# GpSimd's scatters and gathers in both expert layers, without their waits on TensorE's steps

## The chip, the core and the metric

The kernel runs on one core of a Trainium2 chip. TensorE (PE), VectorE (DVE), ScalarE (ACT) and GpSimd (POOL) compute, and transfers run on 16 DMA engines. They are issued by SyncE (SP) and, where rows are picked by an index in memory, by GpSimd as indirect DMAs. The metric is the device time of one execution in microseconds, the median over the runs shown.

## The reference

Sixteen sequences of 512 tokens with 256 features go through four layers, each added to its input after a layer norm: attention a, a mixture of experts, attention b, and the same mixture of experts again. The expert layer, cut to what matters here:

```python
logits = flat @ Wg.T                       # 16 experts
topk_idx, topk_w = _route(sigmoid(logits), bias_corr)   # 4 experts per token
hid = relu(flat @ W1[e].T) ** 2
y = hid @ W2[e].T
out = sum over the token's 4 experts of topk_w * y
shared = relu(flat @ Ws1.T) ** 2 @ Ws2.T
return out + shared
```

## The kernel before

The program has four phases behind one another, with a barrier between them: `phase_a` (attention a), `phase_f` (first expert layer), `phase_b` (attention b, with the routing of the second expert layer) and `phase_e` (second expert layer). In the profiled execution `phase_f` takes roughly from 805 to 1440 us and `phase_e` from 2127 us to the end.

An expert layer computes only the chosen experts. The rows of a sequence are copied to `slots` in DRAM, sorted by expert (a scatter), the sorted rows are worked on in steps of 4 tiles of 128 rows, the results go to `made` in DRAM, and each token's four results are fetched back (a gather), weighted and added by VectorE (`combine`). A block is 128 tokens; a block's scatter or gather is 4 indirect DMAs of 128 rows of 1 KB, one for each of the 4 chosen experts. A sequence has 4 blocks.

One step `v` of tiles is, over the engines:

- SP: `load_tiles(v)` brings 512 KB of `slots` to `xg` (4 buffers), `store_tiles(v)` brings 512 KB of `ye` (2 buffers) to `made`. Both stand in one order in SP's queue, so that a load waits behind the store in front of it.
- PE: `tile_turn(v)` transposes to `XT`, `tile_hidden(v)` makes `Z` (semaphore `ze_done`), `tile_made(v)` makes `Y` (`ye_done`).
- ACT and DVE: copies of expert weights to `wt`, of `XT` to `xe`, relu and square of `Z`, copies of `Y` to `ye`.

Each engine runs the same hand-written loop over slots of time `T`. In slot `T`, step `v = T - E_AT` stands on PE as turn of `v + 1`, hidden of `v`, made of `v - 1`; `E_AT` is 18 in `phase_f` and 2 in `phase_e`. Work of the router, of the shared expert and the combining is put in fixed slots between. Nothing but semaphores keeps the engines in the same slot.

`phase_f` has 84 steps, in 5 groups of sequences (2, 2, 4, 4, 4). When a group is routed, VectorE writes its positions (`pack`, semaphore `packed`, L1391), and GpSimd scatters its blocks, one per slot `T` of `LOT_AT`. The gathers of sequences 0 and 1 are done here too, in the slots from `G_AT`, the ones of the others in `phase_b`. In `phase_f` the waits at issue are `in_step` (on the router's products in the slots ahead of the first step of tiles) and `in_pairs` (two DMAs after `ze_done` of the step, two after `ye_done` of the step before).

`phase_e` has 80 steps in 4 groups of 20. Three groups are already scattered in `phase_b`; the last one's 16 blocks are loaded to `f_st` at the start (L2579) and scattered in two of three slots from `T` = 3 to `T` = 25. Sequence `s` is gathered in the slots `C_AT + 5 s` and the three behind it (`C_AT` = 24), and combined two slots later (L2746). A gather waits for `c_step`, the combining of the same block of the sequence before, since they share the buffer `yg`. The first gather of a group waits until all steps of the group are stored (`ye_stored`). The shared expert of each sequence stands in the same five slots on PE (L2772, L2782, L2791).

The combining is ahead of the square (L2731) and of the copy of `Y` (L2737) in VectorE's slot: where `combine` waits for a gather, the step's own work on VectorE waits behind it, and TensorE's `Y` behind that.

Of the kernel before, what the change touches and what calls it, by code (L numbers as in the profile page):

```python
# [15 lines left out]
KT = H // P  # L16
SEQ = 512
TB = SEQ // P
# [51 lines left out]
EXPERTS, GROUPS, TOP_GROUPS, TOP_K, SCALE = 16, 4, 2, 4, 2.5  # L70
# [14 lines left out]
PER_SEQ = NSTEP // BATCH  # L85
DUO = 2
# [762 lines left out]
def phase_f(nc, tag, shared_c, routes, x_in, base_d, slots, made, w_gate, bias_corr, w_exp, nseq):  # L849

    NP = nseq // DUO
    NV = sum(STEPS1)
    PS = 6
# [8 lines left out]
    E_AT = max(LOT_AT[TB * (FIRST1[n] + SIZES1[n]) - 1] + 3 - STEP1_AT[n] for n in range(len(SIZES1)))  # L862
# [5 lines left out]
    with ExitStack() as ctx:  # L868
# [65 lines left out]
        def used(sem, ring, i):  # L934

            return sem[i % ring], 16 * (i // ring + 1)
# [27 lines left out]
        with nc.Block() as block:  # L964
# [61 lines left out]
            def _(pool):  # L1026
                def scatter(s, b, ks):
                    if s == FIRST1[GROUP1[s]] and b == 0 and ks[0] == 0:
                        pool.wait_ge(packed, GROUP1[s] + 1)
                    for k in ks:  # L1030
                        i = s * PICKS + b * TOP_K + k
                        nc.gpsimd.indirect_dma_start(  # L1032
                            out=slots[GROUP1[s]][:, :], out_offset=bass.IndirectOffsetOnAxis(ap=picks[:, i:i + 1], axis=0),
                            in_=xn[:, s % XN, b, :], in_offset=None).then_inc(scattered[s % XN], 16)
# [24 lines left out]
                def gather(s, b, ks):  # L1059
                    if s == 0 and b == 0 and ks[0] == 0:  # L1060
                        for i in range(2):
                            pool.wait_ge(ye_stored[i], 16 * STEPS1[0] // 2)
                        for i in range(XIN):
                            pool.wait_ge(*used(b_stored, XIN, nseq - XIN + i))
                    if s:
                        pool.wait_ge(c_step, TOP_K * (b + 1))
                    for k in ks:
                        i = s * PICKS + b * TOP_K + k
                        nc.gpsimd.indirect_dma_start(
                            out=yg[:, b, k, :], out_offset=None, in_=made[0][:, :],  # L1070
                            in_offset=bass.IndirectOffsetOnAxis(ap=picks[:, i:i + 1], axis=0)).then_inc(gathered[b], 16)

                def in_step(T):
                    j, e, v = T // PS, T % PS, T - E_AT
                    if j >= NP:
                        return
                    if e == 0 and j:
                        pool.wait_ge(p_done, j)
                    elif e == 1:
                        pool.wait_ge(t_done, KT * DUO * (j + 1))  # L1080
                    elif e in (2, 4):
                        pool.wait_ge(z_done, 4 * j + e)
                    elif e in (3, 5):
                        pool.wait_ge(y_done, 4 * j + e - 1)

                def in_pairs(v, move):
                    pool.wait_ge(ze_done, v + 1)
                    move(range(0, 2))
                    if v:
                        pool.wait_ge(ye_done, v)  # L1090
                    move(range(2, TOP_K))

                for T in range(NT):
                    v = T - E_AT
                    if T in LOT_AT:
                        s, b = LOT_AT.index(T) // TB, LOT_AT.index(T) % TB
                        if 0 <= v < NV:
                            in_pairs(v, lambda ks: scatter(s, b, ks))
                        else:
                            in_step(T)  # L1100
                            scatter(s, b, range(TOP_K))
                    for s, first in ((0, G_AT), (1, G_AT + TB + 3)):
                        if first <= v < first + TB:
                            in_pairs(v, lambda ks: gather(s, v - first, ks))
                for b in range(TB):
                    pool.wait_ge(gathered[b], 2 * 16 * TOP_K)

# [1373 lines left out]
def phase_e(nc, tag, shared_c, routes, xn_d, scattered_upto, base_d, x_out, slots, made, w_exp, wexp, nseq):  # L2481

    NG = nseq // BATCH
    NV = NSTEP * NG
    E_AT = 2
# [6 lines left out]
    with ExitStack() as ctx:  # L2492
# [50 lines left out]
        with nc.Block() as block:  # L2543
# [57 lines left out]
            @block.gpsimd  # L2601
            def _(pool):
                def scatter(s, b, ks):
                    i = s - scattered_upto
                    if b == 0 and ks[0] == 0:
                        pool.wait_ge(st_loaded[i], 16)
                    for k in ks:
                        j = s * PICKS + b * TOP_K + k
                        nc.gpsimd.indirect_dma_start(  # L2609
                            out=slots[s // BATCH][:, :], out_offset=bass.IndirectOffsetOnAxis(ap=picks[:, j:j + 1], axis=0),  # L2610
                            in_=st[:, i, b, :], in_offset=None).then_inc(scattered[i], 16)

                def gather(s, b, ks):
                    if b == 0 and s % BATCH == 0 and ks[0] == 0:
                        for i in range(2):
                            pool.wait_ge(ye_stored[i], 16 * (NSTEP // 2) * (s // BATCH + 1))
                    if s:
                        pool.wait_ge(c_step, PICKS * (s - 1) + TOP_K * (b + 1))
                    for k in ks:
                        i = s * PICKS + b * TOP_K + k  # L2620
                        nc.gpsimd.indirect_dma_start(  # L2621
                            out=yg[:, b, k, :], out_offset=None, in_=made[s // BATCH][:, :],
                            in_offset=bass.IndirectOffsetOnAxis(ap=picks[:, i:i + 1], axis=0)).then_inc(gathered[b], 16)

                lot = TB * scattered_upto
                for T in range(NT):
                    v, w = T - E_AT, T - C_AT
                    scatters = 0 <= v and v % 3 and lot < TB * nseq
                    gathers = 0 <= w < PER_SEQ * nseq and w % PER_SEQ < TB
                    for half, ks in enumerate((range(0, 2), range(2, TOP_K))):  # L2630
                        if (scatters or gathers) and 0 <= v < NV:
                            if half == 0:
                                pool.wait_ge(ze_done, v + 1)
                            elif v:
                                pool.wait_ge(ye_done, v)
                        if scatters:
                            scatter(lot // TB, lot % TB, ks)
                        if gathers:
                            gather(w // PER_SEQ, w % PER_SEQ, ks)
                    lot += bool(scatters)  # L2640

            @block.scalar
# [276 lines left out]
```

## Time and profile before

| | us |
|---|---|
| median of 3 runs | 2673.39 |
| lowest, highest | 2672.3, 2680.75 |
| profiled execution, device time | 2692.99 |
| its span on the core | 2691.3 |
| TensorE busy | 2349.2 (87%) |
| VectorE busy | 1827.2 (68%) |
| ScalarE busy | 1485.7 (55%) |
| GpSimd busy | 1379.8 (51%) |

The profiled execution is 19.6 us above the median of the runs, and 1.7 us of it lie outside the span. Differences are worked out inside the profiled span and then laid on the median. A busy share over the whole span says little here: what counts is which engine is waited for in each phase.

### The profile page before, as it was taken

What the parts mean: (1) busy time and instruction counts of PE and PEld (TensorE: products, weight loads), DVE (VectorE), ACT (ScalarE), POOL (GpSimd) and SP (SyncE); (2) the same over time, 40 slices, a digit from 0 to 9 for tenths busy, and PEclk for the clock granted to TensorE, in tenths of its full rate; (3) what the DMA queues carried; (4) which work ended last, traced back from release to release, by engine and by line L of the source; (5) the groups of instructions that cost most, each with busy time, mean ns of one, the idle gap of its engine ahead of it and who ended that gap; (6) DMA issues with size and microseconds to landing.
All of it is one profiled execution on the core that took longest, in us unless ns stands there. A gap on an engine that the chain in (4) does not pass through costs nothing. (4 is left out here: it accounts for less than half of the span.)

```text
span 2691.3 us, 50441 instructions
## 1 busy us (share of the span) xinstructions
PE 2349.2 (87%) x15632; PEld 1878.3 (70%) x15632; DVE 1827.2 (68%) x4782; ACT 1485.7 (55%) x2987; POOL 1379.8 (51%) x1593
## 2 busy tenths in 40 slices
PE   5999999999977889989994999999899399999983
PEld 3666666666645677779984777777677298888861
DVE  7776767777637777665555688888786555666654
ACT  3766667676642455457773554444344276666640
POOL 3434435344441735457443544777776165555566
PEclk9999999999987899889997999999999699999996
DMA  5786868778664656559884333445443498888874
GB/s 124 181 211 189 216 163 236 182 194 232 172 170 167 221 182 233 203 199 335 297 294 155 101 106 111 154 154 162 139 149 135 177 314 288 297 307 294 307 250 149
DMA packets 255883, 548.41 MB, mean 204 GB/s; under 512 B 33538, under 2 KB 125700, under 8 KB 254596
## 3 DMA queue, kind: packets, MB, share of 16 engines
q1 hardware_dynamic: 206468, 410.90, 50.1%
q0 software_dynamic: 49152, 134.28, 15.0%
q8 instruction: 131, 2.15, 0.4%
q14 instruction: 132, 1.08, 0.2%
HBM read 267.71 MB, written 276.82 MB: 202 GB/s over the span
## 5 line engine op out<-in xcount | busy, mean ns | idle before, releaser
L395 POOL TENSOR_SCALAR_AFFINE_SELECT a_pt<-a_pt 128x512 f32<-128x512 f32 (+1 forms) x320 | 173.8, 543 | 427.2 <-ACT a_pt L494 426.6
L1032 POOL DMA_INDIRECT slots<-f_xn,k_picks x256 | 261.5, 1021 | 248.2 <-PE f_Z L1540 95.7
L2621 POOL DMA_INDIRECT f_yg<-made,k_picks x256 | 254.5, 994 | 171.5 <-PE f_Z L2814 89.6
L494 ACT ACTIVATE a_pt<-a_S 128x384 f32<-128x384 f32 (+3 forms) x640 | 255.3, 456 | 142.4 <-PE a_S L750 140.9
L1760 POOL DMA_INDIRECT k_yg<-made,k_picks x224 | 224.4, 1002 | 128.1 <-issue 60.8
L629 DVE TENSOR_REDUCE a_mx<-a_FB 128x2 f32<-128x384 f32 (+4 forms) x512 | 271.3, 591 | 17.8 <-PE a_FB L730 17.8
L1770 POOL DMA_INDIRECT slots<-b_staged,k_picks x192 | 195.3, 1017 | 78.3 <-issue 57.9
L728 PE MATMUL a_FB<-a_kb,a_qb 128*128 128x192 bf16 (+4 forms) x1024 | 173.4, 257 | 32.7 <-DVE a_mx L629 24.5
L750 PE MATMUL a_S<-a_qs,a_ks 97*128 97x384 f32 (+3 forms) x640 | 189.4, 377 | 3.3 <-ACT a_pt L494 3.2
L476 ACT ACTIVATE a_qb<-a_qh,a_headmask 128x512 bf16<-128x512 f32 x256 | 182.0, 729 | 0.0
L2746 DVE SCALAR_TENSOR_TENSOR f_cb<-f_yg,k_wall,f_cb 128x256 f32<-128x256 f32 x256 | 124.3, 486 | 83.4 <-DMA f_yg<-made,k_picks 76.2
L2666 ACT COPY f_wt<-f_wexp 128x512 f32 x240 | 147.3, 620 | 57.6 <-issue 30.9
L1147 ACT COPY f_wt<-f_wexp 128x512 f32 x252 | 155.4, 619 | 40.7 <-issue 36.2
L1540 PE MATMUL f_Z<-f_xe,f_wt 128*128 128x128 f32 x1344 | 169.6, 281 | 0.0
L1540 PEld LDWEIGHTS f_Z<-f_xe,f_wt 128*128 128x128 f32 x1344 | 162.6, 198 | 0.1
L1550 PE MATMUL f_Y<-f_wt,f_ge 128*128 128x256 f32 x672 | 160.7, 382 | 0.9 <-DVE f_ye L1417 0.9
L2824 PE MATMUL f_Y<-f_wt,f_ge 128*128 128x256 f32 x640 | 153.2, 383 | 4.5 <-DVE f_ye L2737 4.5
L2814 PE MATMUL f_Z<-f_xe,f_wt 128*128 128x128 f32 x1280 | 156.2, 275 | 0.0
L728 PEld LDWEIGHTS a_FB<-a_kb,a_qb 128*128 128x128 bf16 x1024 | 77.7, 98 | 107.9 <-DVE a_mx L629 70.5
L2814 PEld LDWEIGHTS f_Z<-f_xe,f_wt 128*128 128x128 f32 x1280 | 149.6, 192 | 0.2
L1411 DVE TENSOR_TENSOR f_ge<-f_r 128x512 f32<-128x512 f32 x84 | 58.3, 694 | 122.0 <-ACT f_r L1160 122.0
L2373 PE MATMUL b_Y<-b_wo,b_o 128*128 128x256 f32 x512 | 127.2, 392 | 15.7 <-DVE b_o L2202 15.6
(395 smaller groups left out, 6171.0 us busy)
## 6 DMA issues: line engine op xcount, KB each, us to landing
f_xg<-slots SPq DMA_DIRECT2D x164, 512.0 KB, 6.1
made<-f_ye SPq DMA_DIRECT2D x164, 512.0 KB, 3.9
slots<-a_zeros SPq DMA_DIRECT2D x16, 2560.0 KB, 10.8
a_ks<-turned SPq DMA_DIRECT2D x96, 256.0 KB, 7.6
a_qs<-turned SPq DMA_DIRECT2D x192, 128.0 KB, 8.1
a_xin<-in_x SPq DMA_DIRECT2D x16, 512.0 KB, 14.0
turned<-a_kh SPq DMA_DIRECT2D x32, 256.0 KB, 2.6
turned<-a_kl SPq DMA_DIRECT2D x32, 256.0 KB, 2.9
```

The source lines that it names most:

```text
L395: ins = nc.gpsimd.affine_select(out=v[:, :, 0:P], in_=v[:, :, 0:P], compare_op=ALU.is_ge, fill=0.0, base=0, pattern=[[0, nh], [1, P]], cha ...
L476: nc.scalar.activation(qb16[:, h, :], qh[:, t, :].bitcast(F32), ACT.Copy, scale=headmask[:, h % HT:h % HT + 1]).then_inc(q_masked, 1)
L494: nc.scalar.activation(pt[:, u % 4, b * w:(b + 1) * w], S[:, s_bank[2 * u + b], 0:w], ACT.Exp).then_inc(e_done, 1)
L629: nc.vector.tensor_reduce(mx[:, heads[0]:heads[0] + nh, qb], src[:, 0:nh * n].rearrange("p (h c) -> p h c", c=n), AX.X, ALU.max).then_inc( ...
L728: pe.matmul(o[:, j], qb16[:, h, qb * P:(qb + 1) * P], kb16[:, h // HT, k0:k0 + n], start=(j == 0), stop=False, skip_group_check=True)
L750: ins = pe.matmul(S[:, s_bank[i], 0:nh * n], ks[0:ONES + 1, h // 2, kb * P:(kb + 1) * P], qs[0:ONES + 1, h:h + nh, kb * P:kb * P + n], sta ...
L1032: nc.gpsimd.indirect_dma_start(out=slots[GROUP1[s]][:, :], out_offset=bass.IndirectOffsetOnAxis(ap=picks[:, i:i + 1], axis=0), in_=xn[:, s ...
L1540: ins = pe.matmul(Z[:, b * P:(b + 1) * P], wt[:, v % WT, b, k * P:(k + 1) * P], xe[:, v % 2, k, b * P:(b + 1) * P], start=(k == 0), stop=( ...
L1760: nc.gpsimd.indirect_dma_start(out=yg[:, b, k, :], out_offset=None, in_=made[GROUP1[s]][:, :], in_offset=bass.IndirectOffsetOnAxis(ap=rout ...
L1770: nc.gpsimd.indirect_dma_start(out=slots[s // BATCH][:, :], out_offset=bass.IndirectOffsetOnAxis(ap=picks[:, j:j + 1], axis=0), in_=staged ...
L2621: nc.gpsimd.indirect_dma_start(out=yg[:, b, k, :], out_offset=None, in_=made[s // BATCH][:, :], in_offset=bass.IndirectOffsetOnAxis(ap=pic ...
L2814: ins = pe.matmul(Z[:, b * P:(b + 1) * P], wt[:, v % WT, b, k * P:(k + 1) * P], xe[:, v % 2, k, b * P:(b + 1) * P], start=(k == 0), stop=( ...
```

## The change

All waits of GpSimd on TensorE's products go, in both expert layers. What stays is what the data need: `packed`, `st_loaded`, `ye_stored`, `b_stored` and `c_step`. Four DMAs of a block now stand together. The order of blocks in GpSimd's queue is as before, except that a slot of `phase_e` that has both a scatter and a gather now has the whole scatter first, then the whole gather.

```diff
-                def in_step(T):
-                    j, e, v = T // PS, T % PS, T - E_AT
-                    if j >= NP:
-                        return
-                    if e == 0 and j:
-                        pool.wait_ge(p_done, j)
-                    elif e == 1:
-                        pool.wait_ge(t_done, KT * DUO * (j + 1))
-                    elif e in (2, 4):
-                        pool.wait_ge(z_done, 4 * j + e)
-                    elif e in (3, 5):
-                        pool.wait_ge(y_done, 4 * j + e - 1)
-                def in_pairs(v, move):
-                    pool.wait_ge(ze_done, v + 1)
-                    move(range(0, 2))
-                    if v:
-                        pool.wait_ge(ye_done, v)
-                    move(range(2, TOP_K))
...
-                        if 0 <= v < NV:
-                            in_pairs(v, lambda ks: scatter(s, b, ks))
-                        else:
-                            in_step(T)
-                            scatter(s, b, range(TOP_K))
+                        scatter(s, b, range(TOP_K))
...
-                            in_pairs(v, lambda ks: gather(s, v - first, ks))
+                            gather(s, v - first, range(TOP_K))
...
-                    for half, ks in enumerate((range(0, 2), range(2, TOP_K))):
-                        if (scatters or gathers) and 0 <= v < NV:
-                            if half == 0:
-                                pool.wait_ge(ze_done, v + 1)
-                            elif v:
-                                pool.wait_ge(ye_done, v)
-                        if scatters:
-                            scatter(lot // TB, lot % TB, ks)
-                        if gathers:
-                            gather(w // PER_SEQ, w % PER_SEQ, ks)
+                    if scatters:
+                        scatter(lot // TB, lot % TB, range(TOP_K))
+                    if gathers:
+                        gather(w // PER_SEQ, w % PER_SEQ, range(TOP_K))
```

GpSimd's queue at the start of `phase_e`, before (L2609 is the scatter; the scatters of all four sequences go on like this, two by two):

```order
L2601 UNCONDITIONAL_BRANCH [waits barrier_Pool_Activation_PE_DVE_SP_gather]
L2609 DMA slots<-f_st,k_picks 10240x256 [waits f2_st_loaded0,f2_ze_done]
L2609 DMA slots<-f_st,k_picks 10240x256
L2609 DMA slots<-f_st,k_picks 10240x256 [waits f2_ye_done]
L2609 DMA slots<-f_st,k_picks 10240x256
```

The same place and what follows it in the changed kernel, where the scatter is L2585 and the gather L2597:

```order
L2577 UNCONDITIONAL_BRANCH [waits barrier_Pool_Activation_PE_DVE_SP_gather]
L2585 DMA slots<-f_st,k_picks 10240x256 [waits f2_st_loaded0]
L2585 DMA slots<-f_st,k_picks 10240x256 x15
...
L2585 DMA slots<-f_st,k_picks 10240x256 [waits f2_st_loaded3]
L2585 DMA slots<-f_st,k_picks 10240x256 x11
L2597 DMA f_yg<-made,k_picks 128x256 [waits f2_ye_stored1,f2_ye_stored0]
L2597 DMA f_yg<-made,k_picks 128x256 x3
L2585 DMA slots<-f_st,k_picks 10240x256 x4
L2597 DMA f_yg<-made,k_picks 128x256 x12
```

Sixty scatters now stand ahead of the first gather without a wait on a product; four stand behind that gather's wait on `ye_stored`.

GpSimd's queue around the first gathers of `phase_e`, before (slots 24 and 25; L2621 is the gather):

```order
L2609 DMA slots<-f_st,k_picks 10240x256 [waits f2_ze_done]
L2609 DMA slots<-f_st,k_picks 10240x256
L2621 DMA f_yg<-made,k_picks 128x256 [waits f2_ye_stored1,f2_ye_stored0]
L2621 DMA f_yg<-made,k_picks 128x256
L2609 DMA slots<-f_st,k_picks 10240x256 [waits f2_ye_done]
L2609 DMA slots<-f_st,k_picks 10240x256
L2621 DMA f_yg<-made,k_picks 128x256 x2
L2609 DMA slots<-f_st,k_picks 10240x256 [waits f2_ze_done]
L2609 DMA slots<-f_st,k_picks 10240x256
L2621 DMA f_yg<-made,k_picks 128x256 x2
```

Before, eight scatters stood among the first eight gathers, and the first gather could not issue before `Z` of slot 24; now four stand there, and no product is waited for.

## Rows read from the trace of the kernel before

**Rows 1.** The page's first line.
```profile
span 2691.3 us, 50441 instructions
```

**Rows 2.** Windows: stretch, length, busy PE PEld DVE ACT POOL, PEclk, DMA share, GB/s.
```profile
1200.00:1313.00 113.00, 111.79 (x804) 103.11 (x802) 58.83 (x100) 83.86 (x149) 86.69 (x87) 1.00 0.98 333
2132.00:2140.00 8.00, 0.42 (x2) 0.43 (x3) 0.00 (x0) 0.00 (x0) 0.00 (x0) 0.50 1.04 380
2150.00:2244.00 94.00, 93.03 (x660) 85.12 (x659) 46.70 (x82) 70.84 (x125) 55.28 (x56) 1.00 0.90 308
2280.00:2590.00 310.00, 310.00 (x2009) 273.08 (x2008) 210.15 (x393) 210.10 (x373) 167.50 (x167) 1.00 0.87 298
```

**Rows 3.** Waits of GpSimd: line, released by, us in total, times, longest us.
```profile
POOL slots L1032 <- PE f_Z L1540: 95.7, 24, 10.7
POOL f_yg L2621 <- PE f_Z L2814: 89.6, 20, 6.5
POOL slots L2609 <- PE f_Z L2814: 82.7, 9, 55.6
POOL k_yg L1069 <- PE f_Z L1540: 50.7, 3, 33.5
```

**Rows 4.** Timeline, GpSimd: start, us, line, operation, [idle before, releaser]; first 64 scatters.
```profile
859.54 1.16 POOL L1032 DMA_INDIRECT slots<-f_xn,k_picks  x1 [55.08 <-DVE k_picks L1391]
...
940.97 0.97 POOL L1032 DMA_INDIRECT slots<-f_xn,k_picks  x1 [1.79 <-PE f_Z L1540]
```

**Rows 5.** Landings of the tile loads `f_xg` issued between 1200 and 1313 us.
```profile
DMA to landing us min/median/max: 5.2/6.1/7.4
```

**Rows 6.** The same for the loads issued between 1313 and 1345 us.
```profile
DMA to landing us min/median/max: 3.7/3.9/4.0
```

**Rows 7.** Timeline, SP and PE, at the first gathers of `phase_f`.
```profile
1342.16 2.64 SPq L1020 DMA_DIRECT2D k_xin<-bases  x2
...
1351.35 1.09 PE L1528 MATMUL f_XT<-k_ident,f_xg 128*128 128x128 f32 x8 [2.26 <-DMA f_xg<-slots]
```

**Rows 8.** Timeline, start of `phase_e`.
```profile
2127.73 2.01 SPq L2579 DMA_DIRECT2D f_st<-normalised  x4
...
2139.57 1.97 PE L2802 MATMUL f_XT<-k_ident,f_xg 128*128 128x128 f32 x8 [27.94 <-DMA f_xg<-slots]
...
2149.08 0.97 POOL L2609 DMA_INDIRECT slots<-f_st,k_picks  x1 [55.57 <-PE f_Z L2814]
```

**Rows 9.** Timeline, first gathers of `phase_e`.
```profile
2237.99 0.32 SPq L2560 DMA_DIRECT2D made<-f_ye  x1
...
2249.57 1.12 POOL L2621 DMA_INDIRECT f_yg<-made,k_picks  x1 [0.30 <-DMA made<-f_ye]
...
2270.38 2.07 DVE L2746 SCALAR_TENSOR_TENSOR f_cb<-f_yg,k_wall,f_cb 128x256 f32<-128x256 f32 x4 [6.71 <-DMA f_yg<-made,k_picks]
...
2273.80 3.62 PE L2824 MATMUL f_Y<-f_wt,f_ge 128*128 128x256 f32 x8 [3.46 <-DVE f_ye L2737]
```

**Rows 10.** The page's list of DMA issues; last column us to landing.
```profile
made<-f_ye SPq DMA_DIRECT2D x164, 512.0 KB, 3.9
```

**Rows 11.** Timeline, last step of tiles and the end.
```profile
2593.91 1.97 PE L2824 MATMUL f_Y<-f_wt,f_ge 128*128 128x256 f32 x8 [1.06 <-DVE f_ye L2737]
2595.65 2.07 DVE L2746 SCALAR_TENSOR_TENSOR f_cb<-f_yg,k_wall,f_cb 128x256 f32<-128x256 f32 x4 [1.89 <-DMA f_yg<-made,k_picks]
2597.64 0.68 DVE L2737 COPY f_ye<-f_Y 128x512 f32<-128x512 f32 x1
2602.35 0.95 POOL L2621 DMA_INDIRECT f_yg<-made,k_picks  x1 [0.37 <-issue]
...
2682.35 0.95 POOL L2621 DMA_INDIRECT f_yg<-made,k_picks  x1 [0.30 <-issue]
```

**Rows 12.** Timeline, VectorE's copy of expert weights, apart from and beside indirect DMAs.
```profile
2382.36 0.42 DVE L2718 COPY f_wt<-f_wexp 128x512 f32 x1
...
2582.28 0.60 DVE L2718 COPY f_wt<-f_wexp 128x512 f32 x1
```

## Prediction, written before the changed kernel ran

> **What bounds the kernel now.** I read the list of waits first, and in it GpSimd. Its idle time behind TensorE's `Z` is 318.7 us in all (95.7 + 89.6 + 82.7 + 50.7) [rows 3]. That is what the change removes. The question is who waits for GpSimd. The windows answer it. In the long middle of the second expert layer, 2280 to 2590 us, TensorE is busy 310.00 of 310 us [rows 2]: it waits for nothing, so nothing that GpSimd does sooner can help there. In the stretch 1200 to 1313 us it is busy 111.79 of 113 us, and from 2150 to 2244 us 93.03 of 94 us [rows 2]. GpSimd is on the path in four places only, and I went through them in the timeline: the first scatters of the first layer, the start of the second layer, its first gathers, and its end.
>
> **First scatters of the first layer: no change.** They start when the positions are packed, at 859.54 us, and 64 of them follow one another without a wait on a product; the first such wait stands at 940.97 us [rows 4]. (940.97 - 859.54) / 64 = 1.27 us is the price of one scatter, its 0.3 us gap included. GpSimd is its own bound there, and the removed waits were already met. The first tile loads wait for these scatters as before: 0 us.
>
> **Scatters of the later groups: earlier, in bursts.** A group of 4 sequences is 64 scatters, 64 x 1.27 = 81 us back to back, in place of one block per step. No tile load waited for them before, so coming earlier earns nothing. It could cost, through the DMA engines. The trace has the very case: between 1200 and 1313 us GpSimd was late and scattered without a pause (87 of them, 86.69 us busy of 113), the DMA engines were full (0.98, 333 GB/s), and TensorE was still busy for 99% [rows 2]. A tile load then took 6.1 us to land, 7.4 at most [rows 5], in place of 3.9 without indirect DMAs beside it [rows 6], and none was waited for. So a burst beside full steps costs 0 us, from this row; the other end is a rival below.
>
> **First gathers of the first layer: about -0.8 us.** TensorE waits 2.26 us at 1351.35 us for a tile load [rows 7]. SP had two other loads (`k_xin`, 2.64 us of issue, 1 MB) in front of it, and the gathers that had waited up to 33.5 us [rows 3] started just then. Moved, they leave the engines to the load. It is the smaller of the two causes: from rows 5 and 6 the most that indirect DMAs cost a load is 6.1 - 3.9 = 2.2 us, but only the last 3 of its some 6 us were shared, hence between 0 and -2.2, and I take -0.8. If the whole wait went, the half clock behind it would go too (below, 1.7 us), so the far end is -4.
>
> **Start of the second layer: about +2.9 us.** The four loads of `f_st` are issued from 2127.73 us, ahead of the first tile loads, and TensorE starts at 2139.57 us when the first tile load lands [rows 8]. In between the DMA engines are full, 1.04 at 380 GB/s, and GpSimd does nothing [rows 2], since its first scatter waits for `Z` until 2149.08 us [rows 8]. Now it scatters as soon as the first `f_st` load is there, 3.7 us [rows 6] after its issue at the soonest, about 2132. One scatter is 131 KB each 1.27 us, 103 GB/s. If the engines have 380 GB/s for all, the loads keep 277. TensorE needs two tile loads before its first step runs; five more loads of 0.524 MB and one of weights were then still under way ahead of the second one, 3.1 MB: 3.1 MB / 277 GB/s = 11.2 us in place of 8.2, +3.0; I take +2.9. The bounds are 0 (the loads keep their rate) and +4. Everything behind shifts by it. Behind the start the burst goes on to about 2132 + 60 x 1.27 = 2208 us beside full steps; that is the case already priced at 0.
>
> **First gathers of the second layer: -5.4 us.** They need the store of step 19, issued at 2237.99 us [rows 9], landing a median of 3.9 us later [rows 10], at 2242. The first gather started at 2249.57 us, since two scatters stood in front of it that waited for `Z` of slot 24. The view names the store as its releaser, but that had long landed. Then scatters and gathers alternated, and the second block's gather landed only at 2270.38 us, after VectorE had stood still for 6.71 us; TensorE's `Y` waited 3.46 us behind it and ran at the lower clock, 3.62 us [rows 9] for what takes 1.9 us otherwise (an equal group at 2593.91 took 1.97 [rows 11]). In the changed queue: 2242 + 4 gathers + 4 scatters + 4 gathers at 1.27 = 2257, and a landing of some 3.5 us behind the last issue: 2260, ten us before, and 3.7 before VectorE could have used it (2270.38 - 6.71 = 2263.7). The wait goes, and with it 3.5 + 1.7 = 5.2 us, with small change 5.4. What is late next is TensorE itself. If the gate is at 2249.57 us after all, 12 indirect DMAs end the block at 2249.6 + 11 x 1.27 + 3.5 = 2267.1, a gain of 3.3 us in VectorE's wait, and the lower clock perhaps: the bounds are -3.3 and -5.4.
>
> **The end: -2.0 us.** The last 64 gathers need the store of the last step. They run back to back from 2602.35 to 2682.35 us [rows 11], 63 x 1.27 = 80.0 us, and no wait of them is touched. Only their start can move. The store follows VectorE's copy at 2597.64 us, which stands behind a `combine` that waited 1.89 us for a gather; that gather was held back by `Z`. `Y` itself was made by 2593.91 + 1.97 = 2595.88 [rows 11]. With the gathers of that sequence long done, the copy starts at about 2595.9: -1.7 us, and some tenths for a landing with no gathers beside it, -2.0. Before, GpSimd arrived with its own queue at the same moment (gap 0.37 in place of 0.30 [rows 11]), so both had to move; both do. Bounds -1 and -3.
>
> **Steady steps, VectorE.** Beside an indirect DMA VectorE's copy of weights takes up to 0.60 in place of 0.42 us [rows 12], 0.18 more. Before, the pairs were issued at fixed points of the step; now they fall anywhere. 80 steps x 0.18 = 14 us of VectorE at most, hidden under 100 us in which it is idle from 2280 to 2590 [rows 2]. Zero on the path. The Trainium skill, page "SBUF — State Buffer", section "Who interferes with whom", says that GpSimd and VectorE share a port pair as an exclusive lock and the second to come fully blocks. By that a copy behind an indirect DMA of 0.95 us could wait up to 0.95; over 80 steps that would be an estimate of 76 us of VectorE, less than its idle time, and the sum would stay. The trace shows 0.18.
>
> **Sum** inside the profiled span: 0 + 0 - 0.8 + 2.9 - 5.4 - 2.0 + 0 = -5.3 us, 2691.3 to 2686.0 us [rows 1]; with the 1.7 us outside it, 2687.7. On the median, 2673.4 - 5.3 = 2668.1 us, 0.2% less.
>
> **Rivals.**
>
> *The starts are free and the gains full.* If loads keep their rate beside scatters at 2132 us, and the wait at 1351 us goes whole: -4 - 5.4 - 3 = -12.4, 2661.0. [...] Against it: 380 GB/s at a share of 1.04 looks like a ceiling. Chance 0.25.
>
> *The bursts make tile loads late.* Place: the 14 or so steps from 2140 to 2208 us, when the pipeline is just filled. It decides where landings pass the 7.4 us that were still borne [rows 5]. One late load costs what 1351.35 shows: 2.26 us and 1.7 us at the lower clock, 4 us. Five of them: +20; the wait at the first gathers goes anyway, so 2668.1 + 20 = 2688. Against it stands the stretch from 1200 to 1313 us, with 25 such loads and no wait. Chance 0.08.
>
> *The removed waits were cover for nothing, and the start eats the rest.* The gate at 2249.57 is real (-3.3), start +4, end -1, first layer 0: -0.3, so 2673.1. Chance 0.17.
>
> **How the numbers follow.** The forecast, 2668.1, has 0.50; its own range is +4 - 3.3 - 1 = -0.3 to 0 - 5.4 - 3 - 2.2 = -10.6, so 2662.8 to 2673.1. The free start reaches 2661, the quiet rival 2673; the runs before spread from 2672.3 to 2680.8, which I add in part, since a median of few can lie some us off: 2657 to 2679. That leaves out the late loads (0.08) and some tails. About 0.3% (8 us, below 2665.4 or above 2681.4) is what a measurement can tell from no change. Faster by more: the free start, 0.25, and a small part of the forecast, 0.06: 0.31. Slower by more: 0.08. Within: 0.61.
>
> **What would show it.** In the changed profile: GpSimd's waits on `f_Z` are gone, and its idle time stands behind `k_picks`, `f_cb` and the stores. TensorE's first transpose of the second layer comes 2 to 4 us later after the `f_st` issue than the 11.8 us now (2139.57 - 2127.73). No wait of VectorE over 1 us at the second gathered block, and `Y` there at 1.9 us. The last 64 gathers take 80 us again. From 2280 to 2590 TensorE has no gap. The prediction is wrong if tile loads in the bursts are waited for, or if the stretch of steady steps gets longer.

## The result, and the profile after

| | before | changed |
|---|---|---|
| median of 20 runs, us | 2674.03 | 2666.21 |
| lowest to highest, us | 2668.28 to 2694.31 | 2658.15 to 2675.69 |
| ratio to before (95% interval) | 1 | 0.9965 (0.9951 to 0.9980) |
| span of the profiled execution, us | 2691.3 | 2668.8 |

The change takes 7.8 us off the median. The ratio, which is taken between runs made side by side, gives 0.35%, 9.4 us, and its interval goes from 5.3 to 13.1 us. I had forecast 5.3 us, 0.2%. The spans of the two profiled executions differ by 22.5 us, nearly three times the 7.8; only 8.2 us of that stand in the second expert layer, and most of the rest is not the change, as the second trace of the kernel before shows below.

The page of the changed kernel, first line, and its DMA issues (the line that answers to [rows 10]):

```profile
span 2668.8 us, 50322 instructions
...
made<-f_ye SPq DMA_DIRECT2D x164, 512.0 KB, 4.0
```

The waits of GpSimd, against [rows 3] (line, released by, us in total, times, longest us):

```profile
POOL slots L1032 <- DVE k_picks L1367: 125.0, 4, 53.0
POOL f_yg L2597 <- DVE f_cb L2716: 103.7, 25, 18.2
...
POOL k_yg L1069 <- DVE k_xin L1403: 70.7, 3, 69.7
...
POOL slots L2585 <- DMA f_st<-normalised: 38.0, 1, 38.0
```

No wait on `f_Z` is left. GpSimd is idle about as long as before (1291 us in place of 1312), but behind data: the positions, the combining, the first `f_st` load.

Windows of the changed kernel (columns as in [rows 2]): a burst of scatters in the first layer, the first 8 us after the first scatter of the second, and 310 us of full steps:

```profile
1187.00:1263.00 76.00, 74.37 (x543) 69.47 (x542) 39.78 (x68) 56.93 (x102) 58.02 (x60) 1.00 0.97 333
2117.60:2125.60 8.00, 1.91 (x8) 1.57 (x8) 0.00 (x0) 0.73 (x2) 6.17 (x7) 0.50 1.06 386
2263.00:2573.00 310.00, 309.50 (x2001) 272.39 (x1999) 210.77 (x394) 208.73 (x374) 169.46 (x169) 1.00 0.88 301
```

The steady steps are nearly as full as before (309.50 of 310 us against 310.00 [rows 2]). The burst of the first layer runs at the 333 GB/s and full DMA engines that I had read from [rows 2], with TensorE busy 98% of it.

The first gathers of the second layer, against [rows 9]:

```profile
2226.42 0.98 POOL L2597 DMA_INDIRECT f_yg<-made,k_picks  x1 [30.26 <-DMA made<-f_ye]
...
2248.18 2.03 DVE L2716 SCALAR_TENSOR_TENSOR f_cb<-f_yg,k_wall,f_cb 128x256 f32<-128x256 f32 x4
...
2248.94 1.89 PE L2794 MATMUL f_Y<-f_wt,f_ge 128*128 128x256 f32 x8
```

GpSimd now really waits for a store, 30.26 us: SP issued the store of step 19 at 2222.49 us, 3.9 us before the first gather. And VectorE combines the second block (2248.18) with no wait in front; the `Y` behind it has no wait either and takes 1.89 us, where it waited 3.46 us and took 3.62 before.

The last step of tiles, against [rows 11]:

```profile
2573.31 2.04 DVE L2716 SCALAR_TENSOR_TENSOR f_cb<-f_yg,k_wall,f_cb 128x256 f32<-128x256 f32 x4
2575.54 0.69 DVE L2707 COPY f_ye<-f_Y 128x512 f32<-128x512 f32 x1 [0.19 <-PE f_Y L2794]
...
2580.10 0.95 POOL L2597 DMA_INDIRECT f_yg<-made,k_picks  x1 [15.20 <-DVE f_cb L2716]
...
2659.84 0.95 POOL L2597 DMA_INDIRECT f_yg<-made,k_picks  x1 [0.30 <-issue]
```

The last `combine` ahead of the copy has no wait, the copy waits for `Y` alone (0.19), and GpSimd stood ready for 15.20 us before the last 64 gathers could start, where it had arrived in the same moment. (The row names `f_cb` as the releaser; what the gather waited for last, by the queue, is the store of the last step.) The gathers take 79.7 us, as before.

### The second layer, cut at fixed steps

To compare traces I took the start of the same TensorE transposes (`f_XT` of a step `v`, short XT, by their first weight load) in each trace, from the first load of the phase to the last instruction. The differences between them are below, in us; a time with a plus is counted from that first load. The kernels are explained with their experiments further down. I call a stretch paced where GpSimd still waits for TensorE's products, and free where it does not. In this layer `before`, `before_again` and `first_only` are paced throughout, `end_only` up to its last six steps, `gate_only` but for slots 24 and 25, and `scatters_only` from its last scatter on; the others are free. A trace is one execution.

| kernel | load to XT 0 | XT 0 to 4 | 4 to 17 | 17 to 26 | 26 to 30 | 30 to 79 | 79 to end | sum |
|---|---|---|---|---|---|---|---|---|
| before | 11.8 | 15.0 | 57.6 | 49.2 | 29.7 | 292.7 | 107.6 | 563.5 |
| before_again | 9.8 | 15.9 | 58.8 | 48.6 | 30.0 | 292.7 | 108.8 | 564.6 |
| first_only | 10.7 | 15.6 | 57.1 | 49.3 | 27.7 | 292.8 | 107.6 | 560.8 |
| end_only | 10.0 | 15.9 | 57.4 | 49.4 | 29.6 | 292.7 | 106.1 | 561.2 |
| gate_only | 10.1 | 16.0 | 57.4 | 49.0 | 24.3 | 292.7 | 108.2 | 557.7 |
| changed | 10.2 | 16.6 | 57.8 | 48.1 | 24.3 | 292.8 | 105.4 | 555.3 |
| after_again | 12.4 | 17.4 | 58.2 | 48.2 | 24.3 | 293.1 | 105.5 | 559.1 |
| second_only | 10.3 | 16.1 | 58.9 | 48.2 | 24.3 | 295.0 | 105.9 | 558.7 |
| scatters_only | 10.1 | 16.2 | 58.9 | 48.2 | 24.3 | 292.7 | 108.4 | 558.9 |
| hold_start | 9.7 | 14.6 | 58.0 | 50.8 | 24.3 | 292.7 | 105.1 | 555.2 |
| tiles_first | 3.4 | 19.2 | 57.3 | 49.5 | 24.3 | 292.7 | 105.9 | 552.4 |
| best | 3.3 | 19.5 | 58.2 | 49.1 | 24.3 | 293.0 | 105.6 | 553.0 |
| best_four | 3.2 | 16.6 | 60.6 | 49.3 | 24.3 | 293.0 | 105.4 | 552.5 |

### The profile page after: what moved, and what is told of

The parts are those of the page before. It is cut to its first block and busy times, and to the rows that moved or that the text cites. A ratio compares the mean times of both kernels' runs of the same rounds, so it can differ in the third digit from the quotient of the medians.

```text
span 2668.8 us, 50322 instructions
## 1 busy us (share of the span) xinstructions
PE 2328.2 (87%) x15616; PEld 1870.2 (70%) x15632; DVE 1827.4 (68%) x4782; ACT 1483.0 (56%) x2987; POOL 1377.5 (52%) x1593
## 3 DMA queue, kind: packets, MB, share of 16 engines
q8 instruction: 131, 2.15, 0.3%
q14 instruction: 131, 1.07, 0.1%
## 5 line engine op out<-in xcount | busy, mean ns | idle before, releaser
L2597 POOL DMA_INDIRECT f_yg<-made,k_picks x256 | 255.0, 996 | 204.1 <-DVE f_cb L2716 103.7
L1746 POOL DMA_INDIRECT slots<-b_staged,k_picks x192 | 196.8, 1025 | 79.6 <-issue 57.6
L728 PE MATMUL a_FB<-a_kb,a_qb 128*128 128x192 bf16 (+4 forms) x1008 | 167.3, 255 | 29.6 <-DVE a_mx L629 24.4
L728 PEld LDWEIGHTS a_FB<-a_kb,a_qb 128*128 128x128 bf16 x1024 | 77.8, 98 | 107.6 <-DVE a_mx L629 71.9
```

What stands on the lines that cost most here:

```text
L728: pe.matmul(o[:, j], qb16[:, h, qb * P:(qb + 1) * P], kb16[:, h // HT, k0:k0 + n], start=(j == 0), stop=False, skip_group_check=True)
L1746: nc.gpsimd.indirect_dma_start(out=slots[s // BATCH][:, :], out_offset=bass.IndirectOffsetOnAxis(ap=picks[:, j:j + 1], axis=0), in_=staged ...
L2597: nc.gpsimd.indirect_dma_start(out=yg[:, b, k, :], out_offset=None, in_=made[s // BATCH][:, :], in_offset=bass.IndirectOffsetOnAxis(ap=pic ...
```

## The experiments

My theory after the result: the gain is made at two places of the second layer, the first gathers and the last step, and the bursts cost next to nothing. The rivals: the first layer makes the gain; the store of step 19 was the true gate; the free start costs 3 us that the gains had to pay.

### One layer at a time

Edit of the first run: the changed lines of `phase_e` alone, `phase_f` as before. Of the second: the reverse.

> The change in the second expert layer alone; the first keeps its waits. Theory (the gain sits at the first gathers and at the end of the second layer): nearly the whole gain of the changed kernel, ratio to before 0.997, some 7 to 8 us less. In its trace, counted from the first issue of the f_st loads (2127.73 us before): last XT at some +450 in place of +456.0, end at some +555.5 in place of +563.5. Rival (the gain is made in the first layer, by bursts that end sooner, and the second layer's start eats its own gain): ratio 0.999 to 1.000, end at +561 or later.

Measured: 2666.54 us median of 12 runs against 2673.5, ratio 0.9978 (0.9968 to 0.9989). In the trace, last XT at +452.8, end at +558.7 from the first `f_st` load, both some 3 us later than my theory had them. Of these, 2.2 us stand in the steady steps (295.0 in the table), which the last part comes back to.

> The change in the first expert layer alone. Theory: no TensorE wait there depended on GpSimd but for a part of one, so 0 to 2 us less, ratio 0.999 to 1.000, and the second layer ends at +563.5 us from its first f_st load as before. Rival (the first layer carries the gain): 4 us less or more, ratio 0.998 or below, with the stretch from the first tile turn to the last of the first layer, 518.0 us before and 511.5 in the changed kernel, down by about 6 us.

Measured: 2671.91 us median of 12 runs, ratio 1.0001 (0.9990 to 1.0013). End at +560.8. The stretch of the first layer took 514.3 us, between the 518.0 and 511.5 us of the two kernels, which says nothing: the unchanged kernel's second trace took 7.3 us less there than its first.

The second layer carries the gain: 5.9 us by its ratio, between 2.9 and 8.6. The first layer alone gives nothing that can be measured; my -0.8 us for it cannot be told from 0. The tile load that I had hoped to relieve is waited for as long as before (2.26 us in [rows 7]):

```profile
1336.78 1.09 PE L1504 MATMUL f_XT<-k_ident,f_xg 128*128 128x128 f32 x8 [2.15 <-DMA f_xg<-slots]
```

This is the changed kernel's row. The gathers that used to start beside that load are gone from there, and still it waits 2.15 us. It is so in every trace: 1.96 to 2.25 us in the five with a free first layer and these loads in place, 1.67 to 2.72 us in the six with a paced one. So the gathers are not the cause. The two `k_xin` loads in front of it are left, and a later run confirms them.

### How much two traces of one kernel differ

> The kernel before, unchanged, for a second trace. Its profiled span was 2691.3 us where the median of the runs was 2673 to 2674. Theory: differences that appear ahead of the first changed instruction (the changed kernel's trace is 5.7 us ahead of before's there) belong to the execution, so this trace will differ from the first one by several us in the attention phases and in the first layer, yet by under 1 us from the f_st loads to the end of the second layer: +563.5, first gathers at +121.8, TensorE's wait of 3.46 us at the second gathered block. Rival: the second layer's times vary as much as the change moved them (8 us).

Measured: 2684.35 us device time, span 2682.6. That is 8.7 us less than the first trace, of the same program. From the first `f_st` load to the end: 564.6 us, 1.1 more than the first trace. I had expected under 1 us. By sections the second layer differs by 2 us at its start, by 1.2 us in steps 4 to 17 and again at its end, by 0.3 us at steps 26 to 30 and not at all at steps 30 to 79. The first trace was a long execution ahead of this layer, which it reached 9.7 us later. In this trace too VectorE stood still at the second block:

```profile
2260.53 2.05 DVE L2746 SCALAR_TENSOR_TENSOR f_cb<-f_yg,k_wall,f_cb 128x256 f32<-128x256 f32 x4 [6.64 <-DMA f_yg<-made,k_picks]
```

### The gate alone

```diff
-                        if (scatters or gathers) and 0 <= v < NV:
+                        if (scatters or gathers) and 0 <= v < NV and T not in (24, 25):
```

> The kernel before, with the waits on products dropped in two slots alone, 24 and 25 of the second layer, where the first two blocks are gathered and the last two scattered. Theory (the store of step 19 has landed by some 114 us after the first f_st issue, and only the two scatters that waited for Z of slot 24 held the first gather to +121.8): the first gather issues at +113 to +115, VectorE no longer stands at the second block, and the stretch from XT of step 26 to XT of step 30 falls from 29.7 to 24.3 us. The end moves by the same 5.4 us, to +558; ratio 0.998. Rival (the store really landed at +121.8, as the waits view says): the first gather stays at +121 and the stretch at 27 us or more.

Measured: first gather at +114.1, only the usual 0.30 us behind the scatter in front of it, and steps 26 to 30 in 24.34 us. The median was 2670.23 us against 2672.82, ratio 0.9992 (0.9965 to 1.0018), too wide an interval to tell 5 us. The trace decides. The second block's combine in this kernel:

```profile
2249.02 2.11 DVE L2746 SCALAR_TENSOR_TENSOR f_cb<-f_yg,k_wall,f_cb 128x256 f32<-128x256 f32 x4 [0.64 <-DMA f_yg<-made,k_picks]
...
2249.07 1.89 PE L2824 MATMUL f_Y<-f_wt,f_ge 128*128 128x256 f32 x8
```

6.71 us of waiting are 0.64, and TensorE does not wait. Two slots of 80 make the whole gain of this place, to the hundredth the same 24.34 us as the changed kernel. The rival falls: the store had landed, though the view names it as the releaser of the gather at 2249.57 us [rows 9].

### The end alone

```diff
-                        if (scatters or gathers) and 0 <= v < NV:
+                        if (scatters or gathers) and 0 <= v < 74:
```

> The kernel before, with the waits on products dropped for the last six steps of tiles alone. Theory: the last combine ahead of the last tile's copy no longer waits for its gather, so the last store and the last 64 gathers start about 2 us sooner: from XT of the last step to the end 105.5 us in place of 107.6 (108.8 in the second trace). The stretch at the first gathers stays at 29.7. Rival (GpSimd arrives at the last 64 gathers with its queue full either way): 107.6.

Measured: 2665.79 us (one run), and 106.1 us from the last XT to the end, against 107.6, 108.8, 107.6, 108.2 and 108.4 in the five traces whose end is paced: 1.5 to 2.7 us less. In this trace the copy of the last tile waits for `Y` alone, as in the changed kernel:

```profile
2567.89 2.04 DVE L2746 SCALAR_TENSOR_TENSOR f_cb<-f_yg,k_wall,f_cb 128x256 f32<-128x256 f32 x4
2570.13 0.69 DVE L2737 COPY f_ye<-f_Y 128x512 f32<-128x512 f32 x1 [0.19 <-PE f_Y L2824]
```

The stretch at the first gathers stays at 29.6 us. The rival falls.

### The start

```diff
+                    if T == 3:
+                        pool.wait_ge(ze_done, 2)
                     if scatters:
                         scatter(lot // TB, lot % TB, range(TOP_K))
```

> The changed kernel, with one wait put back: the first scatter of the second layer waits for Z of step 1, so GpSimd is silent while the first tile loads come in. My prediction priced the free start at +2.9 us; by that this kernel gains 2.9: XT of step 4 at +24 from the first f_st issue, end at +552.5. What the changed kernel's trace says (loads kept 334 of 379 GB/s, and step 4 stands at +26.8 in both): nothing, +26 to +27 and end at +555. Since the burst is then some 16 us later and ends later, it may run into the first gathers: bursts of 60 scatters from +20 end at +97, ahead of the gate at +113, so nothing is expected of that.

Measured: 2667.03 us median of 12 runs, ratio 0.9971 (0.9952 to 0.9990), no difference to the changed kernel. XT of step 4 stood at +24.3, which is what my prediction's price asks for, and the end at +555.2, which is what the other theory asks for. Neither settles the price. The held start is 2.5 us shorter to step 4 than the changed kernel's, but the paced kernels, in which GpSimd is silent up to the same place (`Z` of step 1), need 25.7 to 26.8 us, so that much of the 2.5 us can be this one execution. Then steps 17 to 26 take 50.8 in place of 48.1 us. There TensorE waits for a tile load:

```profile
2203.05 1.09 PE L2774 MATMUL f_XT<-k_ident,f_xg 128*128 128x128 f32 x8 [1.77 <-DMA f_xg<-slots]
```

I had expected nothing of the later burst. But it was still running when SP issued, in one go, the first `f_xs` load and this tile load (timeline, SP and GpSimd of this kernel):

```profile
2194.43 0.45 SPq L2542 DMA_DIRECT2D f_xs<-normalised  x1
2194.93 1.02 SPq L2529 DMA_DIRECT2D f_xg<-slots  x1
...
2201.38 0.97 POOL L2585 DMA_INDIRECT slots<-f_st,k_picks  x1 [0.30 <-issue]
```

8.1 us pass from the issue to the transpose (2203.05 - 2194.93), over the 7.4 us that were borne in [rows 5]. This is the late tile load of my second rival, once, at 1.8 us. TensorE's clock stayed full behind it (1.00 from 2190 to 2210 us). In the changed kernel the burst has ended by then: its 60th scatter starts at +81.7, the first `f_xs` load at +90.6.

> The kernel before, with the waits dropped in every slot of the second layer that has a scatter, while slots with a gather alone keep theirs. It shows the free start and the burst without the free gathers behind them. Forecast of the prediction: step 4 is 2.9 us late, XT of step 4 at +29 from the first f_st issue. What the other traces say: +26 to +27, no tile load waited for in the burst (steps 4 to 17 in 57 to 59 us as in the kernel before), the first gathers as in the changed kernel, 24.3 us from step 26 to 30, since both slots with a gather and a scatter lose their waits, and the end as before, 107.6 to 108.8 us from the last XT, end at +558.

Edit: the wait stays only in slots with a gather and no scatter. Measured: 2669.63 us (one run, before beside it 2676.72). XT of step 4 at +26.4, steps 4 to 17 in 58.9 us, steps 26 to 30 in 24.3, last XT to end 108.4, end at +558.9. All as expected.

> The changed kernel, for a second trace. From the first f_st issue: end at +555 to +558 in place of +563.5 and +564.6 in the two traces of before; steps 26 to 30 in 24.3 us, last XT to end 105.4 to 106; step 4 at +26 to +27. A start that costs 2.9 us would show as +29.

Measured: 2668.91 us. XT of step 4 at +29.8 and the end at +559.1, some 3 and 1 us outside what I expected; the rest as expected. No trace with a silent GpSimd started as late. Together: with a free start step 4 stands at +26.8, +26.4, +26.4 and +29.8, mean 27.4; with a silent one at +26.8, +25.7, +26.4, +26.1, +25.8 and, in `hold_start`, +24.3, mean 25.9. So the free start costs about 1.5 us. With a spread of 2.5 and 3.4 us within the two groups, these ten traces exclude neither nothing nor the 2.9 us of the prediction. What repeats is one piece of it: from the first XT to the second pass 2.55 to 2.57 us in all six silent starts and 3.35 to 3.77 us in the four free ones.

Why that piece, and not 2.9? The DMA queues in 8 us from the first free scatter (queue, kind: packets, MB, share of 16 engines), changed kernel:

```profile
q1 hardware_dynamic: 1588, 2.67, 92.3%
q0 software_dynamic: 146, 0.40, 12.8%
```

and of the kernel before in the same 8 us:

```profile
q1 hardware_dynamic: 1667, 3.03, 103.5%
```

The loads moved 2.67 in place of 3.03 MB, so 334 in place of 379 GB/s; the prediction had left them 277. Seven scatters are 0.92 MB, but only 0.40 MB of them had moved by then, since a scatter takes 5.7 us to land there. The next 4.4 us moved the other 0.52 MB, at 418 GB/s in all, where the kernel before moved only 279 GB/s. What stays in all four free traces is the second tile load, which is used 0.8 to 1.2 us later behind the first one.

### Tile loads first

```diff
-                for i, s in enumerate(range(scattered_upto, nseq)):
-                    if i < 4:
-                        sp.dma_start(st[:, i], rows(xn_d, s)).then_inc(st_loaded[i], 16)
                 load_tiles(0)
-                sp.dma_start(wexp[:, EXPERTS:], w_exp[:, EXPERTS:]).then_inc(sw_loaded, 16)
                 load_tiles(1)
                 load_tiles(2)
+                for i, s in enumerate(range(scattered_upto, nseq)):
+                    if i < 4:
+                        sp.dma_start(st[:, i], rows(xn_d, s)).then_inc(st_loaded[i], 16)
+                sp.dma_start(wexp[:, EXPERTS:], w_exp[:, EXPERTS:]).then_inc(sw_loaded, 16)
```

> The changed kernel, with SP's first three tile loads of the second layer issued ahead of the four f_st loads, which are wanted later. Theory (the start of the layer is bound by 2 MB of f_st loads ahead of the first tile load, at 380 GB/s, and bursts of scatters cost full steps nothing): the first XT comes 5 us sooner, 2.1 MB / 380 GB/s = 5.5 us, so +5 in place of +10.2, and the end at +550 in place of +555.3; ratio to before 0.995. Rival (TensorE is held by the weights' copies, or the scatters pushed later run into the gathers): first XT sooner but the first Z or the end where it was, within 1 us, ratio as the changed kernel's 0.9965.

Measured: 2661.27 us median of 6 runs, ratio 0.9960 (0.9947 to 0.9973). The first XT stands 3.4 us behind the first load, 6.8 sooner and sooner than expected (+5), and the sum is 552.4, 2.9 us less than the changed kernel's but 2.4 more than expected. By step 4 only 4.3 of the 6.8 us are left, since the fourth tile load now stands behind the `f_st` loads:

```profile
2105.01 3.87 PE L2772 MATMUL f_XT<-k_ident,f_xg 128*128 128x128 f32 x16 [19.16 <-DMA f_xg<-slots]
...
2118.30 1.31 PE L2772 MATMUL f_XT<-k_ident,f_xg 128*128 128x128 f32 x8 [3.08 <-DMA f_xg<-slots]
```

Steps 17 to 26 lose 1.4 us more; 1.07 us of it is a wait for a tile load, as in `hold_start`. The intervals of this ratio and of the changed kernel's 0.9965 overlap, so it is the trace, one execution, that speaks for the gain.

### A version that beats both

Tile loads first, and in the first layer:

```diff
-                    if v == G_AT - 2:
+                    if v == G_AT - 10:
                         for i in range(XIN):
                             sp.wait_ge(*used(b_stored, XIN, nseq - XIN + i))
-                        for s in range(2):
-                            sp.dma_start(xnext[:, s], rows(base_d, s)).then_inc(next_loaded, 16)
+                    if v in (G_AT - 10, G_AT - 6):
+                        s = int(v == G_AT - 6)
+                        sp.dma_start(xnext[:, s], rows(base_d, s)).then_inc(next_loaded, 16)
```

> The changed kernel with the tile loads ahead of the f_st loads in the second layer, as in the run before, and in the first layer the two k_xin loads pulled apart and ahead, to slots 8 and 4 steps sooner than the second of them stood. Theory: the wait of 2.1 to 2.3 us for a tile load at the first gathers of the first layer goes, with the lower clock behind it 4 us, on top of the 5 of the tile loads first: ratio to before 0.994 to 0.995, some 2658. Rival (each k_xin load makes a tile load late wherever it stands): two waits in place of one, ratio as without this edit, 0.996.

Measured: 2658.88 us median of 6 runs against 2672.82, ratio 0.9938 (0.9914 to 0.9962). In the trace the steps 62 to 68 of the first layer take 26.34 us, all at full pace, in place of 28.7 in the changed kernel, and no tile load is waited for there. So it was the pair of `k_xin` loads that held that tile load. The edit gives 2.4 us, not 4: the lower clock behind the wait in [rows 7] was there in three of the eleven traces with the two loads together. The interval still overlaps the changed kernel's (0.9951 to 0.9980).

```diff
-                load_tiles(0)
-                load_tiles(1)
-                load_tiles(2)
+                for v in range(XG):
+                    load_tiles(v)
...
-                    if 0 <= v and v + 3 < NV:
+                    if 1 <= v and v + 3 < NV:
                         load_tiles(v + 3)
```

> The previous version (tile loads first, k_xin loads apart), with the fourth tile load of the second layer also issued ahead of the f_st loads. In the trace with three tile loads first, TensorE waited 3.08 us for the fourth, which stood behind 2.5 MB of other loads, and ran the next products at the lower clock. Theory: that wait and some 1.4 us at the lower clock go, ratio to before 0.992 to 0.993, and from the first tile load to the end 548 to 549 us in place of 553.0. Rival (the wait moves to the fifth tile load, which comes behind the f_st loads as well): as before this edit, 552 us or more.

Measured: 2656.36 us median of 6 runs against 2673.13, ratio 0.9934 (0.9919 to 0.9949), not to be told from the version before it; its interval lies just below the changed kernel's. The rival held: the wait moved on to the fifth tile load, and the sum of the layer stayed at 552.5.

```profile
2126.86 1.86 PE L2772 MATMUL f_XT<-k_ident,f_xg 128*128 128x128 f32 x8 [2.34 <-DMA f_xg<-slots]
```

These loads bring the same bytes in any order. The fifth tile load was issued behind the `f_st` loads, at 2116.28 us, and the DMA engines were full while it was under way (share 1.07 and 0.99 in the two 8 us from 2115). That they are the bound here is my reading of these rows; no run tests it.

## Why the prediction was right, point by point

- **Steady steps: 0, measured about +0.5.** Steps 30 to 79 take 292.7 or 292.8 us in nine traces of thirteen, paced or free. Three more, all free, took 293.0 or 293.1, and one free trace (second_only) 295.0. The means are 292.7 paced and 293.2 free. The difference has a place: in six of the seven traces that are free here, TensorE's weight load waits once or more for a tile load, 0.2 to 0.6 us in five of them and 2.0 us in second_only, whose matmul row is below. None of the six paced traces has such a wait. This is a wait of the kind that I had named as a sign of being wrong, but a small one. What delays these loads no run separates.

```profile
2391.85 1.09 PE L2796 MATMUL f_XT<-k_ident,f_xg 128*128 128x128 f32 x8 [1.64 <-DMA f_xg<-slots]
```

- **Bursts beside full steps: 0.** Steps 4 to 17 took 57.1 to 58.8 us paced, 57.8 to 58.9 free. That is 0.8 us on the means, within the spread of either group. The stretch 1200 to 1313 us in [rows 2] was the right witness. Steps 17 to 26 gained 0.9 us (48.2 against 49.1), for which the prediction had no term: it said that no tile load waited for these scatters, and missed one. The five traces that are paced here wait 0.30 to 0.97 us for the tile load of step 20, as in this row of the first trace; the four in which the burst starts at once, behind the first `f_st` load, do not wait. There it ends before SP issues the first `f_xs` load, and the other traces bear out that this matters: the wait is back where the burst reaches that load (1.77 us in `hold_start`, 1.07 in `tiles_first`, 0.84 in `best_four`), and absent in `best`, where it ends 1.8 us ahead of it.

```profile
2226.39 1.09 PE L2802 MATMUL f_XT<-k_ident,f_xg 128*128 128x128 f32 x8 [0.69 <-DMA f_xg<-slots]
```

- **First gathers of the second layer: -5.4, measured -5.4 to -5.7** (29.7 or 30.0 to 24.34). Two traces that have only this edit or the whole change agree to 0.01 us. The reading against the named releaser was right. One paced trace (first_only) has 27.67: TensorE stood still there too, as the first window below shows, but the clock stayed at full speed behind it, where it averaged 0.83 from 2270 to 2280 us in the first trace of before. So 3.3 us of the gain are the wait (27.67 - 24.34), and the 2.0 to 2.4 at the lower clock (to 29.6, 29.7 and 30.0) come with most executions, not all. The columns are those of [rows 2]:

```profile
2250.00:2260.00 10.00, 6.90 (x42) 5.47 (x41) 8.24 (x16) 4.91 (x9) 6.25 (x7) 1.00 0.70 222
2260.00:2270.00 10.00, 10.00 (x64) 9.12 (x63) 5.67 (x11) 5.45 (x11) 6.13 (x6) 1.00 0.98 350
```

- **The end: -2.0, measured -2.5** on the means (108.1 paced, 105.6 free with gathers free to the end).
- **The start: +2.9, measured about +1.5, of which 0.8 to 1.2 repeat in every trace.** This is the term that was mis-sized. The step that failed: "If the engines have 380 GB/s for all, the loads keep 277". They kept 334 in the first 8 us. I charged a scatter's bytes to the moment of its issue, but it landed 5.7 us later, and over half of the bytes moved after those 8 us.
- **The first layer: -0.8, measured 0** (ratio 1.0001, 0.9990 to 1.0013). The cause that I had called the larger of the two, the `k_xin` loads, was all of it.
- **VectorE: 0, and right.** The longest copy of weights in the first trace took 0.67 us, not the 0.60 of [rows 12]; 80 x 0.25 = 20 us are still far below its 100 idle ones.

By the sections: +1.5 + 0.8 - 0.9 - 5.5 + 0.5 - 2.5 = -6.1 us for the second layer, against 5.9 (2.9 to 8.6) by the ratio of second_only, and 7.8 by the medians or 9.4 (5.3 to 13.1) by the ratio of the whole change. The prediction had -4.5 for this layer. It was right in the places and signs of its two gains, and the two together came out at -8.0 against -7.4. That the whole gain was larger than forecast is not shown: 5.3 us is the end of the interval. That the total came so near is in part luck, for two errors one way (half of the start's cost never came, and a wait of 0.9 us was overlooked) stand against three the other way (a gain in the first layer that did not exist, 0.8 us beside the burst and 0.5 us in the steady steps). By the ratio the result lies beyond the 0.3% bound, where I had put a chance of 0.31; by the median, 2666.2 against 2665.4, just within it. The rival with free starts and full gains, 12.4 us, counted on 4 us in the first layer that never existed.

## What to carry to other kernels

A wait that paces a queue by another engine's progress is free only while that queue has slack. Look for the few places where it comes due: the first use after a gate, and the last. Two slots of eighty made some 5.5 us of this gain, the largest part. Where a view names a releaser of an instruction, look at the time of the one in front of it in the same queue: here, with the usual gap of 0.3 us, the gather was held by the queue, not by the releaser. When a phase starts on loads, order them by who waits first; here 2 MB that TensorE's first steps did not need stood ahead of what it stood still for.

## What the hardware showed that I had not expected

- Beside full DMA engines the indirect DMAs took less from the ordinary loads than their bytes say at first: the loads kept 334 of 379 GB/s in 8 us, with seven scatters of 131 KB issued in that time and 0.40 of their 0.92 MB moved.
- Two executions of one program differ by 8.7 us in their spans, and all of it stands ahead of the second layer, which took 1.1 us the other way. A change of 5 us is read from sections of two traces (24.34 us in nine of nine free ones), not from their spans; but the section at the start of the phase spread by 3 us within one kernel.
- Indirect DMAs hardly slow VectorE's copies of weights. In the first trace 93 copies started while an indirect DMA of some 0.97 us was running on GpSimd; they took 0.43 us at the median and 0.67 at most, against 0.42 at the median for the 50 copies apart from any.
